# VectorE makes the low half of block 12 ahead of the mask pass in a tile's first slot

## What is computed

```python
h = jnp.maximum(_layernorm(x, axis=-1), 0.0)
scores = jnp.einsum('nd,md->nm', h, ks)
scores = jax.nn.leaky_relu(scores, negative_slope=0.2)
scores = jnp.where(adj > 0, scores, -9e15)
attn = jax.nn.softmax(scores, axis=1)
x = x + jnp.einsum('nm,md->nd', attn, ks)
```

## Time and profile before

| | us |
|---|---|
| median of 3 executions | 1658.87 |
| lowest and highest | 1658.17, 1659.25 |
| the profiled execution, its own time | 1658.6 |
| its span | 1656.8 |

### The profile page before, as it was taken

The page is one execution under the profiler, slowest core; times in us unless marked ns, Lnnn a source line. Parts: engine busy times, 40 slices in busy tenths (PEclk is TensorE's granted clock), DMA queues, the critical chain, the costliest instruction groups (busy, mean ns, idle before and its releaser), DMA issues.

```text
span 1656.8 us, 38135 instructions
## 1 busy us (share of the span) xinstructions
PE 1609.1 (97%) x13442; PEld 1181.7 (71%) x13442; DVE 1491.6 (90%) x2592; ACT 1400.4 (85%) x2081; POOL 1155.8 (70%) x1224
## 2 busy tenths in 40 slices
PE   5699999999999999999999999999999999999999
PEld 3477777777777777777777777777777777777777
DVE  7999899899899899999999999999998998998996
ACT  6688888888888888888888888888888888888887
POOL 1576776776776767767767767767767767767766
PEclk8999999999999999999999999999999999999999
DMA  7799999999999999999999999999999999999996
GB/s 235 196 230 261 253 264 256 248 265 269 249 263 254 254 262 263 253 261 255 254 265 259 253 260 253 264 266 248 262 260 256 263 262 248 268 258 244 272 253 127
DMA packets 641340, 417.78 MB, mean 252 GB/s; under 512 B 551040, under 2 KB 575616, under 8 KB 641152
## 3 DMA queue, kind: packets, MB, share of 16 engines
q1 hardware_dynamic: 641152, 415.34, 103.9%
HBM read 276.82 MB, written 4.19 MB: 170 GB/s over the span
## 4 chain that ended last, share of the span: by engine, by line
PE 70%; DVE 18%; issue 4%; ACT 2%; POOL 1%; DMA 0%; DVEq 0%; POOLq 0%
PE ps_out L386 20%; PE ps_T L371 10%; PE ps_out L387 10%; PE ps_scores L360 10%; PE ps_scores L362 10%; PE ps_scores L361 10%; DVE mask L573 8%; DVE scores L591 5%; DVE probsT_lo L600 2%; ACT probsT_hi L470 2%; DVE hT_hi L516 1%; DVE row_min L606 1%; DVE plain_max L609 1%; POOL keys_in L314 0%; PE ps_out L338 0%
## 5 line engine op out<-in xcount | busy, mean ns | idle before, releaser
L314 POOL TENSOR_TENSOR keys_in<-scores,keys_in 128x512 f16<-128x512 f32 x512 | 652.2, 1274 | 41.4
L591 DVE CUSTOM_DVE_ANT_0 scores<-ps_scores,mask,minus_scale 128x1024 f32<-128x1024 f32 x512 | 652.8, 1275 | 1.4 <-PE ps_scores L362 0.6
L312 POOL CAST keys_in<-scores 128x512 f16<-128x512 f32 x512 | 346.0, 676 | 402.3 <-ACT scores L462 402.0
L462 ACT ACTIVATE scores<-scores,neg_max 128x1024 f32<-128x1024 f32 x512 | 582.5, 1138 | 0.0
L453 ACT ACTIVATE scores<-scores 128x1024 f32<-128x1024 f32 x512 | 537.8, 1050 | 51.9 <-DVE pair_min L591 51.8
L600 DVE TENSOR_TENSOR probsT_lo<-ps_T,probsT_hi 128x512 f16<-128x512 f32 x512 | 350.2, 684 | 130.1 <-ACT probsT_hi L470 130.1
L470 ACT ACTIVATE probsT_hi<-ps_T 128x512 f16<-128x512 f32 x512 | 305.7, 597 | 186.1 <-PE ps_T L371 185.7
L386 PE MATMUL ps_out<-keys,probsT_hi 128*128 128x256 f16 x2048 | 392.8, 272 | 18.8 <-DVE probsT_lo L600 12.8
L360 PE MATMUL ps_scores<-keysT_hi,hT_hi 128*128 128x512 f16 x1024 | 391.2, 382 | 16.4 <-DVE keysT_lo L555 9.4
L361 PE MATMUL ps_scores<-keysT_lo,hT_hi 128*128 128x512 f16 x1024 | 390.5, 381 | 0.0
L362 PE MATMUL ps_scores<-keysT_hi,hT_lo 128*128 128x512 f16 x1024 | 390.1, 381 | 0.0
(11 more groups left out here) (52 smaller groups left out, 830.0 us busy)
## 6 DMA issues: line engine op xcount, KB each, us to landing
adj_in<-in_adj_dram SPq DMA_DIRECT2D x512, 512.0 KB, 5.1
keys_in<-keys_in SPq DMA_TRANSPOSE x512, 4.9
x_in<-in_x_dram SPq DMA_DIRECT2D x64, 64.0 KB, 2.1
keys_in<-in_L_gnn_ks_dram SPq DMA_DIRECT2D x8, 512.0 KB, 7.3
out_dram<-out_tile SPq DMA_DIRECT2D x64, 64.0 KB, 1.8
```

Source lines behind the costliest of these rows:

```text
L314: nc.gpsimd.tensor_tensor(half[:, BLOCK:2 * BLOCK], probs(t, b), half[:, 0:BLOCK], ALU.subtract) \
L462: nc.scalar.activation(s, s, ACT.Exp, bias=neg_max[:, t % 2:t % 2 + 1], scale=-SLOPE, accum_out=pair_sum[:, t % 2, p:p + 1]).then_inc(prob ...
L591: nc.vector.tensor_tensor_reduce(out=score_pair(q, p), in0=ps_scores[:, slots, :].rearrange("p s k -> p (s k)"), in1=mask[:, (p // 2) % 2, ...
```

## The change

In slot 0 the low half (`split_probs_lo`) is issued ahead of `make_mask`. In all other slots the order stays as it was.

```diff
+                    split = behind(i, j, T_LAG, BY_PE, this, prev)
+                    if split and j == 0:
+                        split_probs_lo(*split)
                     if more and j % 4 == 0:
                         make_mask(i + 1, j // 4)
                     if more and j % 2 == 1:
                         add_mask(i + 1, p)
                         if p == PAIRS - 1:
                             minimum(i + 1)
-                    split = behind(i, j, T_LAG, BY_PE, this, prev)
-                    if split:
+                    if split and j > 0:
                         split_probs_lo(*split)
```

## The result

The changed kernel takes 1636.72 us (median of 4, 1636.66 to 1636.72) against 1658.71 us of the kernel before on the same chip. The ratio is 0.9868, with a 95% interval of 0.9854 to 0.9882. It is faster by 22.0 us. The forecast was 1637.2 us.

A forecast was written before the change was run, and what follows sets the result against it. TensorE, with matmuls busy 97% of the span, was taken as the bound. Saving 61 x 0.355 = 21.7 us from 1658.6 gives 1636.9; the median lies 0.27 us higher, so 1637.2 us, range 1634 to 1647.

The forecast's parts named there:

- The wait in slot 2: TensorE's output matmul waits for VectorE's low half, starting 0.79 us after the transposes instead of 0.43; forecast to go.
- The count of 61 tiles: Tiles forecast to gain 0.355 us each: the 62 changed steps less the first, where TensorE has no such wait.
- Step (a): Slot 0: the low half moves forward, waits 0.21 us for ScalarE's high half, and saves TensorE 0.355 us a tile.
- The fourth wait a tile: New VectorE wait of about 0.2 us for the high half, before the low half; four in a tile instead of three.
- Step (b): The mask pass moves back but, held by GpSimd, ends where it did; add_mask starts 0.56 us earlier; path cost 0.
- ScalarE's wait of 0.65 us: In slot 3 ScalarE waits for the masked pair; forecast to shrink from 0.65 to about 0.1 us.
- Step (c): Which engine limits next: VectorE, ScalarE and DMA keep up with TensorE coming 0.36 us earlier; path cost 0.
- The wait for hT_lo: TensorE's wait at the start of a tile, 0.14 us, forecast to stay.
- The rival that ends slower: VectorE becomes the bound through its new head-of-line wait in slot 0: 0.24 us a tile, 1673.5 us; chance 0.04.
- the second bound in (b): The mask pass costs 2.08 us at its new place too; add_mask starts 0.29 us later, TensorE still loses nothing.

## Why the prediction was right

The place and the cause. The wait in slot 2 was put down to the mask pass, and the mask pass's 2.08 us to GpSimd's subtraction. The run with the short subtraction shows both: take that operation away and the pass is 1.23 us, TensorE's wait is gone and 22 us come back with VectorE's order as it was.

The size. 0.355 us a tile was read from start to start; a tile became shorter by 25.033 - 24.675 = 0.358 us. By the idle time printed beside the row, 0.20 us, the gain would have been 12.2 us. It was 22.0. The Trainium skill's warning in Perfetto Trace Analysis, section Identifying the Most-Contended Engine, that matmul busy time misleads because matmuls are pipelined, holds for idle time too: the row before reaches over the gap, and hides 0.16 us of it. The count of 61 tiles gives 21.8 us with 0.358, against 21.9 between the two spans.

Step (a). The low half was to wait 0.21 us and start at 808.16 on the clock of before, 0.21 behind the end of the row maximum. It waits 0.20 us and starts at 798.15, 0.21 behind it. The fourth wait a tile is in the counts: 255 waits of the low half for ScalarE in place of 195, 60 more.

Step (b), the one small miss. The pass was to end where it ended, and it does: 1.08 us behind GpSimd in both traces. But add_mask was to start with it, 0.03 us ahead of its end, and starts 0.13 us behind it (800.13 against 800.00). Behind the old pass stood the low half, which does not read the mask; now add_mask follows directly, and it needs the mask that the pass writes. In the list of after this is 9.7 us of idle time in front of L591, in place of 1.4. So VectorE is early in slot 1 by 0.38 us (2.34 us behind neg_max in place of 2.72) and not by 0.56: ScalarE's wait of 0.65 us shrank to 0.29 and not to 0.1. It costs nothing, since none of it is on the path.

Step (c), who is next. Nobody, up to the 0.358 us: the chain is 93% TensorE. The wait for hT_lo stayed, as said, and the run that removes it after the change shows that the next 0.145 us could be had as well. The same edit on the kernel before shows what the prediction had not asked: that wait, although printed in each tile, was worth nothing until slot 2 was mended.

The rival that ends slower had its price from 0.24 us a tile and its point of decision from VectorE's slack. In slot 0 the head-of-line wait is 0.20 us and is absorbed. With the exchange in all four slots the tile takes 26.59 us (transposes of h at 102.22 and 1697.87, again 60 tiles), mostly by passes that GpSimd holds. That a pass is held at its new place too is the second bound in (b) of the prediction; this rival had no term for it.

## What to carry to other kernels

When a short operation that another engine waits for stands behind a long one that can itself be held up, exchange them if the short one's input is ready early (0.2 us of waiting here), and look at where the long one lands: three further exchanges, which put it under the operation that holds it, cost 7% against the changed kernel. Read what a wait of TensorE costs from start to start against the same pair of instructions elsewhere. Of two waits in one period, the later one may be pinned by a chain that starts ahead of the earlier. Here mending the earlier alone gave nothing, and behind the mending of the later it gave 9.5 us.

## What the runs showed of the hardware

GpSimd's subtraction and this mask pass (int32 in, bf16 out, both in SBUF) do not run at the same time. A pass of 1.22 us that meets a running subtraction ends 1.08 to 1.09 us behind it: 809.99 against 808.91 before the change, 800.00 against 798.92 after it, 810.47 against 809.38 where all slots were exchanged. The held time stands inside the row of the pass, which looks like a slow instruction. It works the other way too, in the changed kernel: a pass that starts at 791.18 is followed on GpSimd by a subtraction of 2.02 us in place of 1.16:

```profile
791.18 1.34 DVE L573 TENSOR_SCALAR mask<-adj_in 128x2048 bf16<-128x2048 int32 x1
```

```profile
791.53 2.02 POOL L314 TENSOR_TENSOR keys_in<-scores,keys_in 128x512 f16<-128x512 f32 x1
```

The low half, which reads one operand from PSUM and one from SBUF, is not held: its 512 rows in the changed kernel lie between 676 and 694 ns. The Trainium skill, SBUF — State Buffer, section SBUF: two separate sides, says that VectorE and GpSimd share a pair of ports that the first to start holds for its whole instruction, against VectorE operations in a two-port mode or with two SBUF inputs (the latter only where GpSimd's operation reads SBUF). The rows so far agree with it. The pass has one SBUF input, so by that page it would have to run in a two-port mode; no run here shows its mode.

One pair of rows of the changed kernel does not fit the words "first to start", if the start of a row is meant:

```profile
809.23 1.84 POOL L300 TENSOR_SCALAR x_norm<-x_in,mean_var,rstd 128x128 f32<-128x128 f32 x1
```

```profile
809.71 1.22 DVE L573 TENSOR_SCALAR mask<-adj_in 128x2048 bf16<-128x2048 int32 x1
```

GpSimd's x_norm starts 0.48 us ahead of the pass, and yet the pass takes its usual 1.22 us and x_norm 1.84, where it takes 0.80 when no pass falls into it (at 833.91). Here GpSimd gives way although its row began first. Why is not shown.
